# A graph network kernel: one list of ids by slot in place of ids loaded per slot, deeper rings, and a rewritten GRU stage

## The reference, cut to what matters

```
feat_in, feat_out = x @ W_in.T + b_in, x @ W_out.T + b_out
a_in  = mean over edges into a node (dst) of feat_in[src]
a_out = mean over edges out of a node (src) of feat_out[dst]
h = gru_cell(concat(a_in, a_out), x, ...)     # sigmoid, sigmoid, tanh
x = layernorm(x + h)
```

## Time and profile before

| | us |
|---|---|
| three runs | 23025.8, 23088.97 (median), 23107.62 |
| profiled execution | 23050.08 |
| its span | 23048.5 |
| busy PE / weight loads / DVE / ACT / POOL | 12864.9 / 9943.0 / 8520.6 / 3852.9 / 9828.0 |
| granted PE clock, mean | 0.681 |

### The profile page before, as it was taken

How to read it: one execution, slowest core, us unless ns; L and a number is a source line. 1 busy time by engine, 2 the same in 40 slices (tenths; PEclk the granted TensorE clock), 3 DMA queues, 4 the chain that set the end, 5 groups by cost and what they waited for, 6 DMA issues and landing times. The chain is left out here.

```text
span 23048.5 us, 371307 instructions
## 1 busy us (share of the span) xinstructions
PE 12864.9 (56%) x76034; PEld 9943.0 (43%) x76035; DVE 8520.6 (37%) x33126; ACT 3852.9 (17%) x9613; POOL 9828.0 (43%) x10418
## 2 busy tenths in 40 slices
PE   3444443444444444445555556777777777777773
PEld 2222223333333333335555544555555555555552
DVE  4333343332333333335545544333333333333333
ACT  0000001111111111100000002233333333333331
POOL 2444444444444444444444420344444444444440
PEclk9655556666666666667777778677677777777775
DMA  6222222222222222234444430111111131111131
GB/s 231 35 35 35 37 42 56 69 68 68 68 69 68 69 68 68 68 84 113 114 113 114 114 73 15 43 44 44 45 44 45 44 44 45 45 45 45 44 44 30
DMA packets 3234314, 1465.86 MB, mean 64 GB/s; under 512 B 2388398, under 2 KB 3029362, under 8 KB 3233775
## 3 DMA queue, kind: packets, MB, share of 16 engines
q1 hardware_dynamic: 2794486, 548.09, 12.8%
q0 software_dynamic: 386304, 796.93, 12.7%
q10 hardware_dynamic: 53492, 120.52, 1.5%
HBM read 1108.06 MB, written 467.75 MB: 68 GB/s over the span
## 5 line engine op out<-in xcount | busy, mean ns | idle before, releaser
L1522 POOL DMA_INDIRECT ring<-q_rows,small x3556 | 3369.8, 948 | 4597.3 <-ACT ring L1616 3609.8
L1562 PE MATMUL bank<-w,ring 64*128 64x129 f32 x7112 | 2334.8, 420 | 2074.4 <-DVE ring L1476 1183.7
L1562 PEld LDWEIGHTS bank<-w,ring 64*128 64x128 f32 x7112 | 1450.0, 254 | 2754.8 <-issue 1323.8
L876 PE MATMUL bank<-ident_b,ring 128*128 128x128 bf16 x3332 | 489.1, 298 | 3578.9 <-DVE ring L825 2241.1
L698 POOL DMA_INDIRECT ring<-in_x,small x1664 | 1572.5, 945 | 1926.7 <-DVE small L595 1276.3
L1080 POOL DMA_INDIRECT ring<-in_x,small x1664 | 1572.1, 945 | 1889.4 <-DVE small L1016 1244.4
L1475 DVE TENSOR_TENSOR ring<-bank,ring 128x256 f32<-128x256 f32 x1778 | 729.7, 419 | 4387.0 <-DMA edges_b<-ring,small 3651.7
L945 POOL DMA_INDIRECT edges_a<-ring,small x1664 | 1598.3, 961 | 1750.9 <-ACT ring L933 1300.5
L945 POOL DMA_INDIRECT edges_b<-ring,small x1664 | 1598.3, 961 | 1664.6 <-ACT ring L933 1212.7
L1100 PE MATMUL bank<-p,ring 128*128 128x129 f32 x8320 | 1482.8, 342 | 1463.7 <-issue 986.1
L1100 PEld LDWEIGHTS bank<-p,ring 128*128 128x128 f32 x8320 | 1387.3, 255 | 1505.3 <-issue 1505.2
(11 more groups left out here) (249 smaller groups left out, 23114.3 us busy)
## 6 DMA issues: line engine op xcount, KB each, us to landing
p<-edges_b SPq DMA_DIRECT2D x525, 262.0 KB
p<-edges_a SPq DMA_DIRECT2D x520, 262.0 KB
ring<-ids_by_dst SPq DMA_DIRECT2D x8360, 1.0 KB
ring<-bonds_by_dst SPq DMA_DIRECT2D x3328, 32.0 KB
bonds_by_dst<-in_bond ACTq DMA_DIRECT2D x5, 20625.0 KB
ring<-edges_a SPq DMA_DIRECT2D x1792, 33.0 KB
ring<-edges_b SPq DMA_DIRECT2D x1776, 33.0 KB
ring<-q_rows,small POOLq DMA_INDIRECT x3556
```

What stands on the lines that cost most here:

```text
L1522: pool.indirect_dma_start(out=gath[:, k, 0:D], out_offset=None, in_=c.q_dram, in_offset=bass.IndirectOffsetOnAxis(ap=gidx[g][:, k % HALF:k ...
L1562: nc.tensor.matmul(out, bond, c.weight(W_1C, D + 1, BOND), start=True, stop=False, skip_group_check=True)
```

## The change

It adds a stage `list_ids_by_slot` between `sort_by_dst` and the first sum. In nine steps, of 3 x 128 slots each, POOL gathers the ids of 128 slots at a time, one slot (1 KB, 128 pairs) per partition; DVE casts them to fp32, PE transposes them so that a slot's 128 edges lie along the partitions, and DVE computes seven planes of 8 values per group: two digits of the source block, gather index, row within the block, source block, src and dst. SP writes the planes to DRAM (`dst_slot_ids`, 56 words per partition and group).

- The first sum loads planes with two DMAs per group (this group, and the digits of the group of the other half), 8 groups ahead; DVE only makes one-hots (8 x 128, and two of 13 and two of 8 columns per slot for the counts, crossed by PE); POOL takes the index from the loaded plane and gathers into a ring of 32 slots; SP reads no slot starts.
- The sort has 32 record buffers in place of 16, one list load per group, three groups ahead, and bonds two groups ahead. SP's wait for ACT's copies stands ahead of them.
- The second sum has one list load per step, seven ahead, and a ring of 32 gathers. A new wait on all inner sums of the step before stands between the windows and the list load. The windows keep their two sets.
- The gate loop: the means move to ACT with reciprocals made once for all blocks; the has-rows and biases become bf16 in three pieces with 9 rows, so that the transpose and two products of them are bf16; x is loaded 7 blocks ahead; PE does the transposes of block b + 1 before the gates of block b; the loop body has 14 blocks instead of 2; the GRU arithmetic is two fused operations and a subtraction in place of four. The bias pieces go through three small DMAs ahead of the loop.
- The split loop: the first piece, q and the second piece are copied by ACT, the rest stays on DVE; the bias product has bf16 rows and a bank of its own is used for q; normalise runs two blocks ahead.

```diff
+XFROM = 19
+XSLOTS = 7
+RINGW = 10528
+GROUPS_D, B_GROUP, PLANES = SG * P // HALF, HS // HALF, 7
+SRC_HI, SRC_LO, GATHER, LOCAL, BUCKET, SRC, DST = range(PLANES)
+TRIO = 3
+GRPS = 4
+DEEP = GRPS * HALF
+LOOK = 2 * GRPS
...
+        self.slots_d = dram("dst_slot_ids", [P, GROUPS_D, PLANES * HALF])
...
+def list_ids_by_slot(c):
     nc = c.nc
+    s_tab, s_raw, s_cast, s_turned = c.sem("l_tables"), c.sems("l_raw_in", 2), c.sem("l_cast"), c.sem("l_turned")
+    s_dst, s_step, s_made, s_out = c.sem("l_dst_copied"), c.sem("l_steps"), c.sem("l_made"), c.sems("l_out", 2)
+    STEPS, W = SG // TRIO, TRIO * P
...
     with nc.Block() as block:
         @block.sync
         def _(sp):
+            with nc.allow_non_contiguous_dma(reason="one start per partition"):
+                sp.dma_start(starts, c.d_tables[0].rearrange("o (s p) -> p (o s)", p=P)).then_inc(s_tab, 16)
+            sp.dma_start(blocks, c.d_tables[2].to_broadcast([P, SCOLS])).then_inc(s_tab, 16)
+            for t in range(STEPS):
+                sp.wait_ge(s_made, 4 * t + 4)
+                sp.dma_start(c.slots_d[:, t * (W // HALF):(t + 1) * (W // HALF), :],
+                             lists[t % 2].rearrange("p g f k -> p g (f k)")).then_inc(s_out[t % 2], 16)
+            for n in range(2):
+                sp.wait_ge(s_out[n], 16 * ((STEPS + 1 - n) // 2))
+        @block.gpsimd
+        def _(pool):
+            pool.wait_ge(s_tab, 32)
+            for t in range(STEPS):
+                if t >= 2:
+                    pool.wait_ge(s_cast, t - 1)
+                for j in range(TRIO):
+                    pool.indirect_dma_start(
+                        out=raw[t % 2][:, j * 2 * P:(j + 1) * 2 * P], out_offset=None, in_=runs,
+                        in_offset=bass.IndirectOffsetOnAxis(ap=starts[:, t * TRIO + j:t * TRIO + j + 1], axis=0),
+                    ).then_inc(s_raw[t % 2], 16)
         @block.vector
         def _(dve):
             step = Chain(dve, s_step)
+            def cast(t):
+                dve.wait_ge(s_raw[t % 2], 16 * TRIO * (t // 2 + 1))
+                if t >= 2:
+                    dve.wait_ge(s_turned, t - 1)
+                nc.vector.tensor_copy(ids[t % 2], raw[t % 2].rearrange("p (s e k) -> p s k e", s=TRIO, k=2)).then_inc(s_cast, 1)
+            dve.wait_ge(s_tab, 32)
+            cast(0)
+            for t in range(STEPS):
+                if t + 1 < STEPS:
+                    cast(t + 1)
+                plane = lambda k: lists[t % 2][:, :, k, :]
+                dve.wait_ge(s_dst, t + 1)
+                if t >= 2:
+                    dve.wait_ge(s_out[t % 2], 16 * (t // 2))
+                if t:
+                    dve.wait_ge(s_made, 4 * t)
+                step.link(nc.vector.tensor_tensor(plane(LOCAL), plane(DST), grouped(blocks[:, t * W:(t + 1) * W]), ALU.subtract))
+                step.link(nc.vector.tensor_scalar(late, plane(LOCAL), float(P), float(SRC_NONE), ALU.is_ge, ALU.mult))
+                step.link(nc.vector.tensor_tensor(plane(SRC), grouped(turned[0][t % 2]), late, ALU.max))
+                step.mark(nc.vector.tensor_copy(whole, plane(SRC)))
+                nc.vector.tensor_scalar(plane(GATHER).bitcast(I32), plane(SRC), float(N - 1), None, ALU.min).then_inc(s_made, 1)
+                step.wait()
+                nc.vector.tensor_scalar(plane(BUCKET).bitcast(I32), whole, 7, None, ALU.logical_shift_right).then_inc(s_made, 1)
+                nc.vector.tensor_scalar(plane(SRC_HI).bitcast(I32), whole, 10, None, ALU.logical_shift_right).then_inc(s_made, 1)
+                nc.vector.tensor_scalar(plane(SRC_LO).bitcast(I32), whole, 7, 7, ALU.logical_shift_right,
+                                        ALU.bitwise_and).then_inc(s_made, 1)
+        @block.tensor
+        def _(pe):
+            for t in range(STEPS):
+                pe.wait_ge(s_cast, t + 1)
+                if t >= 2:
+                    pe.wait_ge(s_made, 4 * (t - 1))
+                for j in range(TRIO):
+                    for k in range(2):
+                        last = nc.tensor.transpose(turned[k][t % 2][:, j * P:(j + 1) * P], ids[t % 2][:, j, k, :], c.ident)
+                last.then_inc(s_turned, 1)
+        @block.scalar
+        def _(act):
+            for t in range(STEPS):
+                act.wait_ge(s_turned, t + 1)
+                if t >= 2:
+                    act.wait_ge(s_out[t % 2], 16 * (t // 2))
+                nc.scalar.copy(lists[t % 2][:, :, DST, :], grouped(turned[1][t % 2])).then_inc(s_dst, 1)
...
+            def load_ids(u, g):
+                sp.dma_start(ids[g][:, 0:4, :].rearrange("p f k -> p (f k)"), c.slots_d[:, bass.ds(u, 1), 0:4 * HALF]
+                             .rearrange("p o w -> p (o w)")).then_inc(s_ids[g], 16)
+                sp.dma_start(ids[g][:, 4:6, :].rearrange("p f k -> p (f k)"), c.slots_d[:, bass.ds(u + B_GROUP, 1), 0:2 * HALF]
+                             .rearrange("p o w -> p (o w)")).then_inc(s_ids[g], 16)
+            for g in range(LOOK):
+                load_ids(g, g)
+            sp.dma_start(c.tab[D_BLOCKS:D_BLOCKS + 1, 0:SCOLS], c.d_tables[1]).then_inc(s_tab, 16)
+            sp.dma_start(c.tab[D_STARTS:D_STARTS + 1, 0:SCOLS], c.d_tables[0]).then_inc(s_tab, 16)
+            with sp.Fori(0, TURNS_P) as i:
+                for g in range(LOOK):
+                    sp.wait_ge(s_acc, i * (LOOK * HALF) + (HALF * (g + 1) + 2 * BANKS))
+                    load_ids(i * LOOK + (g + LOOK), g)
...
+            def mark(i, g, ahead=0):
+                u = i * LOOK + (LOOK * ahead + g)
+                dve.wait_ge(s_ids[g], 32 * i + (32 * ahead + 32))
+                local = ids[g][:, LOCAL, :]
+                nc.vector.tensor_tensor(hot[g % 2], local.unsqueeze(2).to_broadcast([P, HALF, P]),
                                         c.iota_p.unsqueeze(1).to_broadcast([P, HALF, P]), ALU.is_equal).then_inc(s_hot, 1)
+                dve.wait_ge(s_digits_read, u + 1)
+                for hot_d, plane, width in ((his[g % 2], SRC_HI, HU), (los[g % 2], SRC_LO, HV)):
+                    for s in range(2):
+                        digit = ids[g][:, plane + 4 * s, :].bitcast(I32)
+                        nc.vector.tensor_tensor(hot_d[:, s, :, :], digit.unsqueeze(2).to_broadcast([P, HALF, width]),
+                                                c.iota_p[:, 0:width].unsqueeze(1).to_broadcast([P, HALF, width]),
+                                                ALU.is_equal).then_inc(s_digits, 1)
...
+            with pool.Fori(0, TURNS_P) as i:
+                for g in range(LOOK):
+                    u = i * LOOK + g
+                    pool.wait_ge(s_ids[g], 32 * i + 32)
+                    pool.wait_ge(s_agg, u * PAIRS + PAIRS)
                     pool.sem_inc(s_go, 1)
+                    for k in range(HALF):
+                        at = g % GRPS * HALF + k
                         pool.indirect_dma_start(
+                            out=gath[:, at, 0:D], out_offset=None, in_=c.ins["x"],
+                            in_offset=bass.IndirectOffsetOnAxis(ap=ids[g][:, GATHER, k:k + 1].bitcast(I32), axis=0),
+                        ).then_inc(s_g[at], 16)
...
+            def load_bonds(u, g, turn):
+                starts = slot_values(c, mybir.EngineType.SP, D_STARTS, u * HALF, HALF)
                 for k, start in zip(range(g * HALF, (g + 1) * HALF), starts):
+                    sp.wait_ge(s_sc[k], turn)
                     sp.dma_start(rec[:, k, 0:BOND], c.bond_d[bass.ds(start, P), :]).then_inc(s_bond[k], 16)
+            for g in range(3):
+                sp.dma_start(ids[g].rearrange("p f k -> p (f k)"), c.slots_d[:, g, LOCAL * HALF:PLANES * HALF]).then_inc(s_ids[g], 16)
+            for k in range(2):
+                sp.wait_ge(c.s_copy[k], 16)
+            for g in range(2):
+                load_bonds(g, g, 0)
             for part in range(SPARTS):
+                if part:
+                    sp.wait_ge(c.s_copy[part + 1], 16)
+                with sp.Fori(part * (TURNS_R // SPARTS), (part + 1) * (TURNS_R // SPARTS)) as i:
+                    for g in range(GRPS):
+                        u = i * GRPS + g
+                        sp.wait_ge(s_xv, u * 4 + 3)
+                        sp.dma_start(ids[(g + 3) % GRPS].rearrange("p f k -> p (f k)"),
+                                     c.slots_d[:, bass.ds(u + 3, 1), LOCAL * HALF:PLANES * HALF]
+                                     .rearrange("p o w -> p (o w)")).then_inc(s_ids[(g + 3) % GRPS], 16)
+                        load_bonds(u + 2, (g + 2) % GRPS, 16 * i + 16 * ((g + 2) // GRPS))
...
+                with sp.Fori(n * (QSTEPS // 2 // LOOK), (n + 1) * (QSTEPS // 2 // LOOK)) as i:
+                    for g in range(LOOK):
+                        u = i * LOOK + g
+                        load_windows(u, g % 2, edges)
+                        sp.wait_ge(s_agg_in, u * PAIRS + GRPS * PAIRS)
+                        load_ids(u + LOOK - 1, (g + LOOK - 1) % LOOK)
...
+            def gru(i, j):
```

(35 more changed lines are left out.)

829 lines of the change are left out of this document (399 added, 430 removed).

## The result

The changed kernel took 20763.22 us (median of 4 runs, 20736.7 to 20776.92) against 23098.29 for the kernel before (4 runs) on the same chip. The ratio is 0.8994 (95% interval 0.8973 to 0.9014). It is faster by 10.1%, and 2123 us slower than the forecast of 18640, outside its range.

What follows compares the result with a forecast made beforehand. SP's queue, slowed by POOL, was taken as the bound. First sum with list -1124, sort -1994, second sum -974, node update -271 and -83 make -4446 from 23050.08: 18604, or 18640 as median; range 17850 to 19600.

Steps and rivals of the forecast that it cites:

- What bounds the kernel: SP's load queue is the bound: about 0.52 us a load with POOL quiet, 1.12 us beside it.
- Both are under POOL's 10.0, with gathers 32 deep, so POOL ends last: First sum: DVE and PE need less than POOL's 10.0 us a group; 2250 us with the list, -1124.
- T = 9 (0.52 + 0.6 x 10.1/T) + 1.2: Sort: nine SP loads and one slot read set 10.9 us a group; 4549 us, -1994.
- hides with nothing to spare: Second sum: SP's new wait on inner sums costs nothing, its round trip being about 12.1 us; group 11.9 us.
- rival (b): Coupled waits of SP and PE at half clock: sort 12.0 and second sum 14 us a group, 19530 us; chance 0.20.
- 1.0 us clear and 2.15 beside POOL: Second sum: price of each of SP's five window loads, with POOL quiet and with POOL issuing.
- the 0.3 us taken off: Second sum: 12.2 us a group lowered to 11.9, because the same sum gave 17.8 before where 16.7 was measured.
- Node update: Gate loop 3.9 us a block, 417 us (-271); split loop 2.4 us a block, 240 us (-83).
- the 1% that the forecast allowed: Messages: unedited, change 0; the forecast is wrong if they move by more than 1%.
- List: New stage: 25 us and 14 us at most of table loads, nine steps of 8 us; 110 us, ends 80 and 190.
- (a): POOL's pace everywhere, SP slowed by its number of loads: sort 4217, second sum 2160 us, total 17970; chance 0.14.
- (c): SP's new waits put load and use in a row: sort 19, second sum 24.2 us a group, 24500 us; chance 0.01.

Runs made afterwards that it cites:

- b_both: Changed kernel with second-sum ids asked one group less ahead, loop bodies of 4 there, POOL 16 slots ahead in the first sum; 14499 us.
- b_spaced: Changed kernel with four empty semaphore instructions on POOL after every gather and scatter; 14539 us.
- a_half: Changed kernel without every second gather of both sums and every second bond load of the sort; 17543 us.
- b_pause: Changed kernel with POOL waiting for its last transfer after every 8 gathers of the first sum and every 4 scatters of the sort; 16948 us.
- c_before: Kernel before, unchanged, on another chip than the result's group; 21848 us (7 runs).
- c_both: Same edits to the changed kernel as b_both, on the chip of c_before; 19857 us, 0.9096 of the kernel before.
- a_narrow: Changed kernel with 4 bytes per index in place of 512 in both sums' gathers, and a fixed block read by PE in the sort; 20149 us.
- a_free: Changed kernel with DVE adding into fixed blocks in the first sum and second-sum ids asked one group less far ahead; 20044 us.
- a_look4: Changed kernel with second-sum loop bodies of 4 steps in place of 8, ids asked three steps ahead instead of seven; 20137 us.
- c_after: Changed kernel, unchanged, on the chip of c_before; 19887 us (4 runs), 0.9085 of the kernel before.
- the three groups with steps (result, a and c): Sets of runs on different chips where small queue instructions often took 0.55 to 0.8 us; kernel before 23098, 22064 and 21848 us.

## Why the prediction was wrong, by its own steps

**What bounds the kernel.** That SP's queue was full and slowed while POOL issued was right for the chip that was measured. It was taken for a fixed price, 0.52 and 1.12 us a load, and it goes with the steps: without them the loads are 0.5 us apart beside POOL too, and the kernel before already runs its first sum, sort and second sum at 11.1, 10.2 and 11.0 us a group (2314/208, 4244/416, 2293/208).

**First sum, the step that failed first:** "Both are under POOL's 10.0, with gathers 32 deep, so POOL ends last". The forecast knew from its own rows that POOL's issuing slows a queue, charged it to SP, and let DVE and PE work at their old pace beside a POOL that no longer pauses; this slowing of DVE and PE is a term that the sum had at nothing. The group took 11.9 us where the sum had 10.0. Without steps it took 10.2, 2124 us (b_both) and 2129 (b_spaced), where the forecast had 2140, so the term is 1.7 us a group; with half of the gathers the group took 6.4 (a_half). There was a sign of it in the trace before: of DVE's 17 steps there, seven lie in the one burst that ran on past 10 us (2798.9 to 2806.7), and the others one each near 6 us into a burst of 8.

**Sort:** the step "T = 9 (0.52 + 0.6 x 10.1/T) + 1.2" failed, because SP is not what ends last. a_half showed it. In the changed kernel POOL waits for ACT, ACT for PE's products, and these come 0.7 us and more apart late in a burst: the chain PE, ACT, DVE that makes POOL's next positions takes 13.05 us a group, where the sum had 10.9. That this chain ends last is read from the waits and from the runs without steps, where POOL is the last with 10.16; no edit made the chain alone faster.

**Second sum:** the round trip that "hides with nothing to spare" doesn't hide. In the waits of SP's queue the load of ids (line 1064) stands 728.8 us behind PE's inner sums, 3.5 us for each group of 8 slots, and 5 windows take up to 9.76 us, about as before:

```profile
SPq L1064 <- PE bank L1193: 728.8, 206, 9.0
9799.73 9.76 SPq L1073 DMA_DIRECT2D p<-edges_a  x5
```

A group takes 15.5 us where the sum had 11.9; rival (b) had 14. Easing the wait gave 3.4%, loop bodies of 4 groups 4.7%, both together 3.8%. The windows were read as a transfer's cost, 1.0 us clear and 2.15 beside POOL. Without steps five of them take 3.75 us beside an issuing POOL (b_pause), and a group 10.4 us (2168/208). Two slips are in the sum itself. (9.62 - 0.5)/4 is 2.3 and not 2.4 us. And with 8 id loads in place of 1 its stated terms give 16.9 for the kernel before, not 17.8, so that the 0.3 us taken off had no ground; both are small beside the miss.

**Node update:** -312 us against -354 forecast, and -310 to -316 on the other chips, with steps or without. The first and last sigmoid of the gate loop and the first and last product of the split loop:

```profile
L1500 ACT ACTIVATE ring<-bank x98: 356/383/384, 11440.9 to 11775.0; 128x256 f32<-128x256 f32 x98
L1458 PE MATMUL bank<-w,ring x196: 421/502/582, 11781.7 to 12105.3; 128*128 128x128 f32 x196
```

The first line holds 97 distances between blocks, 3.44 us each, where 3.9 was forecast. The split loop gained next to nothing: 3.33 us a block, where 2.4 was forecast and 3.30 (323/98) measured before; PE is busy 179 of its 316 us, so PE's product was not the bound. The products and the transpose that became bf16 (lines 1430, 1433 and 1408) take 76.5 us against 149.1, half off and not three quarters.

**Messages:** not edited, +231, outside the 1% that the forecast allowed. The same code took 4566 to 4587 us in all the runs without steps and 7253 to 8206 with them, and with them its time rises nearly in order with the number of SP's steps in the stage:

| run | SP's steps | messages, us |
|---|---|---|
| c_before | 561 | 7253 |
| a_half | 661 | 7331 |
| c_both | 740 | 7434 |
| a_narrow | 837 | 7701 |
| a_free | 849 | 7673 |
| a_look4 | 876 | 7795 |
| c_after | 882 | 7730 |
| before | 961 | 7975 |
| after | 1076 | 8206 |

So the spread goes with the steps. Why their number differs from kernel to kernel in a stage that none of them edits, and so whether the change moved it at all, stays open; the changed kernel is the longer one on both chips where both kernels were traced.

**List:** 65 us, not 110, below the lower bound of 80. Which of its terms was too dear was not looked into.

**The rivals.** (b) was right in kind for the second sum and too small. (a), POOL's pace everywhere, gives the stages of a chip without steps: it had 4217 for the sort (4227) and 2160 for the second sum (2168). The first follows from its mechanism; the second is luck, since it let DVE hold the stage at 10.3 us, and in b_pause POOL issues through the stage with a single hole. The rule cited for it, the Trainium skill's "DMA: Bandwidth & Descriptors", section "SWDGE vs HWDGE vs iDMA", read as independence of the queues, agrees with the chips without steps (3.95 us for SP's eight loads) and not with the others (8.22). (c) fell. The gain depends on the steps as much as the time does. Without steps the changed kernel's stages add up to about 14520 us: 14497 of b_both, 29 more for the second sum as it is in b_pause and some 5 less for the node update. Against 15117 that is a ratio of 0.961: about 315 us of the 597 are the node update, 125 the first sum with the list, 125 the second sum, 17 the sort. The changed kernel itself was not run whole on such a chip.

**Open: what the steps are.** Shown: they come only in stages in which POOL has indirect transfers under way, they get fewer with half as many gathers (248 in place of 1060 on DVE in the first sum), and they don't mind the bytes or the kind of instruction. In the traces with steps, records of semaphores are missing. A gather tells of its landing with 16 such records (26559 for 1664 gathers in b_both's first sum). Of 1349 gathers of the first sum 114 have none of the 16, and 399 of 3076 scatters in the sort; before it was 281 of 1336 and 673 of 2551. Without steps each has some (of 1349, 3159, 1270 and 3243). Counted over all semaphores the loss is larger. Records in each stage:

| stage | changed kernel, with steps | b_pause, without |
|---|---|---|
| first sum | 6380 | 37858 |
| sort | 32679 | 124200 |
| second sum | 13134 | 51064 |
| node update | 7697 | 7701 |
| messages | 64810 | 124164 |

Instructions are not missing: the rows of the stages count the same number of PE's and POOL's, with steps and without. Two things follow. Where a trace with steps names no releaser ("issue", "remote"), the record of it may be what is missing, so such idle time is less sure than its length. And the steps go together with a path on which the chip writes its records. The Trainium skill ("NOTIFIC — the notification-queue block", section "Overflow: three behaviours, one of which stalls the engine") says that the block's own pipeline holds its producers back rather than lose a record inside it. The steps, with complete instruction records, would fit such holding back; the missing semaphore records do not follow from that sentence. Whether the writing of records makes the steps, or both come from something else on the chip, no run here tells: every run has a granted clock of its own on record, so in none were the records taken away. Pauses and fewer indices were run without steps only, so they were not tried on the question.

## What to carry to other kernels

Before pricing a change, look at the least and the longest duration of the queue's small instructions (57/57/65 in b_both, 1/57/1408 in the changed kernel with steps). Where they differ much, something holds the queues back, and a gain on paper that lets POOL run on without pause can be partly given back by its neighbours. A duration that depends on which engine is busy may be the chip's and not the operation's: run the kernel before on a second chip before building a model on it. When the slowed instructions of a queue are taken away and only the name of the idle time changes, as in a_free, those instructions were not the cause.

## What was not expected of the hardware

The kernel before takes 15101 to 15137 us on four chips and 21848 to 23098 in the three groups with steps (result, a and c). PE's work in the unedited messages is 4338 us busy of 4571 at a granted clock of 0.97 without steps, and 5757 of 8206 at 0.72 with them: of the 3635 us that the stage is longer, 1419 (5757 - 4338) are PE's own busy time, and they stand beside a mean granted clock of 0.72, between its two levels (1.2 and 2.4 GHz), in place of nearly always the upper. What came first, PE's pauses or the clock, no run tells. Loop bodies of 8 groups in the second sum are fetched again in every turn (six pieces of 8 KB in 124 us), those of 4 groups are not (6 pieces in the whole stage); without steps that was worth 29 us at most.
